# A gated cross-attention and int8 layer on one core: the order of the last step, and who makes the last batch's scales

## The reference, cut to what matters

```python
x = x + tanh(g_xattn) * cross_attention(layernorm(x), ctx)     # 16 batches, 512 rows of 512, 16 heads, 120 keys
# then, with layernorm(x) as z, row by row:
amax    = max(abs(z), axis=-1)
x_scale = maximum(amax, 1e-6) / 127
z_q     = round(z / x_scale)                                    # int8
ffn     = (z_q @ weight_q.T) * x_scale * weight_scale + bias
x = x + tanh(g_ffn) * ffn
```

## Time and profile before

| | |
|---|---|
| median of three executions | 811.59 us (811.49 to 811.66) |
| the profiled execution's own time | 812.33 us |
| its span | 810.4 us |
| PE busy | 794.0 us (98%) |
| DVE busy | 582.8 us (72%) |
| ACT busy | 556.1 us (69%) |
| POOL busy | 523.7 us (65%) |

### The profile page before, as it was taken

How to read it: one execution, slowest core, us unless ns; L and a number is a source line. 1 busy time by engine, 2 the same in 40 slices (tenths; PEclk the granted TensorE clock), 3 DMA queues, 4 the chain that set the end, 5 groups by cost and what they waited for, 6 DMA issues and landing times.

```text
span 810.4 us, 17171 instructions
## 1 busy us (share of the span) xinstructions
PE 794.0 (98%) x6658; PEld 522.4 (64%) x6658; DVE 582.8 (72%) x916; ACT 556.1 (69%) x845; POOL 523.7 (65%) x518
## 2 busy tenths in 40 slices
PE   8899999999999999999999999999999999999995
PEld 5665666666666766667667666667667666666563
DVE  4877788676767768678676767768578666767768
ACT  5676577675776667676676776667677675777685
POOL 4626484775947568494685947568495775845687
PEclk9999999999999999999999999999999999999999
DMA  8632604242141422314242161323414141111112
GB/s 278 231 69 90 200 28 124 73 154 75 40 160 62 137 79 72 125 53 142 74 140 70 41 186 53 118 80 82 133 54 123 61 117 54 53 40 53 53 52 104
DMA packets 39632, 79.68 MB, mean 98 GB/s; under 512 B 6913, under 2 KB 8321, under 8 KB 37505
## 3 DMA queue, kind: packets, MB, share of 16 engines
q1 hardware_dynamic: 38976, 77.75, 30.2%
q10 hardware_dynamic: 576, 0.85, 0.3%
HBM read 61.78 MB, written 16.81 MB: 97 GB/s over the span
## 4 chain that ended last, share of the span: by engine, by line
PE 88%; DVE 5%; issue 2%; POOL 1%; ACT 1%; DMA 1%; SPq 0%; DVEq 0%; ACTq 0%; POOLq 0%
PE bank_b L340 29%; PE bank_a L340 19%; PE scores L395 8%; PE sum_ps L426 7%; PE scores L412 7%; PE pv_ps L430 6%; PE bank_a L474 5%; PE scores L417 2%; PE bank_b L474 2%; DVE row_max L1092 2%; PE bank_a L449 1%; PE sum_ps L403 1%; DMA wk_stage<-in_wk 1%; DVE q_lo L1103 1%; PE scores L370 1%
## 5 line engine op out<-in xcount | busy, mean ns | idle before, releaser
L1092 DVE TENSOR_REDUCE row_max<-scores 128x16 f32<-128x1920 f32 x64 | 138.0, 2157 | 125.7 <-PE scores L395 125.7
L1433 POOL TENSOR_TENSOR o_lo<-on,o_hi 128x512 fp32r<-128x512 f32 x48 | 68.5, 1427 | 130.6 <-ACT o_hi L788 130.6
L770 ACT ACTIVATE probs<-scores 120x2048 f32<-120x2048 f32 x64 | 120.5, 1882 | 39.7 <-PE scores L417 39.7
L1441 POOL TENSOR_TENSOR x<-x,gbias_r 128x512 f32<-128x512 f32 x64 | 82.1, 1284 | 26.3 <-ACT cen L794 25.2
L395 PEld LDWEIGHTS scores<-k_sb,q_sb 32*128 32x128 f32 x2048 | 62.9, 186 | 53.0 <-issue 52.3
L1399 POOL TENSOR_TENSOR xt<-xt,rstd_b 128x512 f32<-128x512 f32 x60 | 91.4, 1571 | 2.4 <-ACT rstd_b L1026 2.1
L1429 POOL TENSOR_TENSOR x<-x,gbo_r 128x512 f32<-128x512 f32 x64 | 83.9, 1323 | 2.1 <-DMA x<-in_x 2.0
L788 ACT ACTIVATE o_hi<-on 128x512 fp32r<-128x512 f32 x48 | 30.3, 632 | 72.9 <-DVE on L1113 72.9
L340 PE MATMUL bank_b<-xt_hi,wq_hi 128*128 128x512 f32 x188 | 79.4, 422 | 0.5 <-DVE xt_lo L1082 0.5
L1446 POOL TENSOR_TENSOR x<-x,u_sb 128x512 f32<-128x512 f32 x56 | 73.6, 1315 | 7.9 <-DVE u_sb L1181 7.9
L395 PE MATMUL scores<-k_sb,q_sb 32*128 32x120 f32 x2048 | 74.7, 282 | 1.3 <-issue 0.9
(11 more groups left out here) (222 smaller groups left out, 1973.8 us busy)
## 6 DMA issues: line engine op xcount, KB each, us to landing
xt<-in_x_t SPq DMA_DIRECT2D x16, 1024.0 KB, 6.3
x<-in_x SPq DMA_DIRECT2D x64, 256.0 KB, 2.9
out_x<-x SPq DMA_DIRECT2D x61, 256.0 KB, 2.0
x_in<-in_x SPq DMA_DIRECT2D x60, 256.0 KB, 3.4
rstd_b<-rstd_rows SPq DMA_DIRECT2D x14, 256.0 KB, 4.7
ctx_sb<-in_ctx_t SPq DMA_DIRECT2D x8, 360.0 KB, 4.7
probs<-in_wq SPq DMA_DIRECT2D x4, 256.0 KB, 4.3
x<-in_wo SPq DMA_DIRECT2D x1, 1024.0 KB, 9.3
```

Source lines behind the costliest of these rows:

```text
L770: act.activation(probs[0:KEYS], scores[0:KEYS], ACT.Exp, scale=SCALE).then_inc(p_ready, 1)
L1092: dve.tensor_reduce(row_max[:].rearrange("p (t r) j -> p r t j", r=ROWG)[:, :, :, j], scores[:, :, 0:QT * KEYS].rearrange("p r (t k) -> p ...
L1433: pool.tensor_tensor(o_lo[i % 2][j], on[:], o_hi[i % 2][j].bitcast(F32), ALU.subtract).then_inc(o_split, 1)
L1441: pool.tensor_tensor(x1_of(m)[:, t], x1_of(m)[:, t], gbias_r[:], ALU.add).then_inc(x1b_ready, 1)
```

## The change

Five edits, all in the last step and in what follows it:

- PE: tile 1's chunk 2 moves from ahead of the wait for `o_last_split` to behind it; tile 0's chunk 3 is now the first work behind the wait, and then come tile 1's chunks 2 and 3.
- POOL, last step: `x1_deviations(m, 1)` is put ahead of `add_out(e, 3)`; `bias_x1(m, 3)` goes ahead of `bias_x(i, 2)`; `bias_x(i, 3)` leaves the step and is done behind `deviation_last(1)`.
- POOL makes one more value in `deviation_last`: `floor_last` = (var + eps) * rstd * 1e-6.
- DVE's `quant_factors_last` makes `q_unit` = max(amax, floor) / 127 and its reciprocal `q_rec`, two instructions for three.
- `xs_last` = q_unit * rstd * 127 is made by POOL in a new `unit_last`, for all four tiles between the last `bias_x1` and the first `add_own`.

```diff
--- before.py
+++ after.py
@@ -102,7 +102,7 @@
         x1_stat, x1_mv = sb("x1_stat", [P, QT, 6]), sb("x1_mv", [P, QT, 2])
         x1_var, x1_rstd, x1_std = sb("x1_var", [P, QT]), sb("x1_rstd", [P, QT]), sb("x1_std", [P, QT])
         q_amax, q_xs, q_unit, q_rec = (sb(f"q_{s}", [P, QT]) for s in ("amax", "xs", "unit", "rec"))
-        xs_last, rec_last = sb("xs_last", [P, QT]), sb("rec_last", [P, QT])
+        xs_last, floor_last = sb("xs_last", [P, QT]), sb("floor_last", [P, QT])
         cen = sb("cen", [P, 2, D + 1])
         u_sb = sb("u_sb", [P, D])
         z_b = [sb(f"z_b{i}", [P, D], BF16) for i in range(2)]
@@ -158,7 +158,7 @@
         ffn_done, u_ready = sem("ffn_done"), sem("u_ready")
         x1b_ready, out_ready = sem("x1b_ready"), sem("out_ready")
         o_last_split, last_pool, last_steps = sem("o_last_split"), sem("last_pool"), sem("last_steps")
-        last_xs = sem("last_xs")
+        last_xs, last_units = sem("last_xs"), sem("last_units")
         last_turned, last_zt, last_out = sem("last_turned"), sem("last_zt"), sem("last_out")
         last_stored = sem("last_stored")
 
@@ -630,12 +630,15 @@
                 pe.wait_ge(u_ready, nth(e, QT, 3))
                 turn_z(m, 0, bank_b)
                 pe.wait_ge(o_split, nth(i, DT, 2))
-                for t in range(2):
-                    for c in range(DT - 1):
-                        add_heads(i, t, c, scores[:, t])
+                for c in range(DT - 1):
+                    add_heads(i, 0, c, scores[:, 0])
+                for c in range(DT - 2):
+                    add_heads(i, 1, c, scores[:, 1])
                 pe.wait_ge(o_last_split, 1)
-                for t in range(2):
-                    add_heads(i, t, DT - 1, scores[:, t]).then_inc(proj_done, 1)
+                add_heads(i, 0, DT - 1, scores[:, 0]).then_inc(proj_done, 1)
+                for c in range(DT - 2, DT):
+                    ins = add_heads(i, 1, c, scores[:, 1])
+                ins.then_inc(proj_done, 1)
                 project_o(i, 2, scores[:, 2])
                 pe.wait_ge(log_done, nth(i, DT, 3))
                 turn_z(m, 1, sum_ps)
@@ -811,7 +814,7 @@
                                bias=x1_mv[:, t, 0:1]).then_inc(cen_ready, 1)
 
             def round_last(t):
-                act.wait_ge(last_steps, nth(t, 2, 1))
+                act.wait_ge(last_steps, t + 1)
                 act.activation(cen_last[t], cen_last[t], ACT.Identity, scale=q_rec[:, t:t + 1],
                                bias=magic[:]).then_inc(scaled, 1)
 
@@ -1150,13 +1153,11 @@
 
             def quant_factors_last(t):
                 one = slice(t, t + 1)
-                dve.wait_ge(last_pool, nth(t, 2, 1))
+                dve.wait_ge(last_pool, nth(t, 3, 2))
                 dve.wait_ge(amax_done, nth(LAST, QT, t))
-                dve.tensor_scalar(xs_last[:, one], q_amax[:, one], x1_rstd[:, one], Q_EPS, ALU.mult, ALU.max).then_inc(last_xs, 1)
-                dve.wait_ge(last_xs, t + 1)
-                dve.reciprocal(rec_last[:, one], xs_last[:, one]).then_inc(last_steps, 1)
-                dve.wait_ge(last_steps, nth(t, 2, 0))
-                dve.tensor_scalar(q_rec[:, one], rec_last[:, one], x1_rstd[:, one], Q_MAX, ALU.mult, ALU.mult).then_inc(last_steps, 1)
+                dve.tensor_scalar(q_unit[:, one], q_amax[:, one], floor_last[:, one], 1.0 / Q_MAX, ALU.max, ALU.mult).then_inc(last_units, 1)
+                dve.wait_ge(last_units, t + 1)
+                dve.reciprocal(q_rec[:, one], q_unit[:, one]).then_inc(last_steps, 1)
 
             def dequantise_own(m, t, bank):
                 dve.wait_ge(ffn_done, nth(m, QT, t))
@@ -1416,8 +1417,15 @@
                 one = slice(t, t + 1)
                 pool.wait_ge(x1_mean, nth(LAST, QT, t))
                 pool.tensor_scalar(x1_var[:, one], x1_mv[:, one, 1], LN_EPS, 1.0, ALU.add, ALU.mult).then_inc(last_pool, 1)
-                pool.wait_ge(last_pool, nth(t, 2, 0))
+                pool.wait_ge(last_pool, nth(t, 3, 0))
                 pool.tensor_tensor(x1_rstd[:, one], x1_var[:, one], half_neg[:, one], ALU.pow).then_inc(last_pool, 1)
+                pool.wait_ge(last_pool, nth(t, 3, 1))
+                pool.tensor_scalar(floor_last[:, one], x1_var[:, one], x1_rstd[:, one], Q_EPS, ALU.mult, ALU.mult).then_inc(last_pool, 1)
+
+            def unit_last(t):
+                one = slice(t, t + 1)
+                pool.wait_ge(last_units, t + 1)
+                pool.tensor_scalar(xs_last[:, one], q_unit[:, one], x1_rstd[:, one], Q_MAX, ALU.mult, ALU.mult).then_inc(last_xs, 1)
 
             def quant_units(m, h):
                 two = slice(2 * h, 2 * h + 2)
@@ -1523,24 +1531,26 @@
                 quant_units(m, 0)
                 bias_x(i, 1)
                 low_o(i, 2)
+                x1_deviations(m, 1)
                 add_out(e, 3)
-                x1_deviations(m, 1)
                 bias_x1(m, 2)
+                bias_x1(m, 3)
                 bias_x(i, 2)
                 quant_units(m, 1)
-                bias_x(i, 3)
-                bias_x1(m, 3)
 
             def turns_and_layers():
                 m = LAST - 1
                 deviation_last(0)
                 deviation_last(1)
+                bias_x(LAST, 3)
                 bias_x1(LAST, 0)
                 bias_x1(LAST, 1)
                 deviation_last(2)
                 deviation_last(3)
                 bias_x1(LAST, 2)
                 bias_x1(LAST, 3)
+                for t in range(QT):
+                    unit_last(t)
                 for t in range(QT):
                     add_own(m, t)
                 add_own(LAST, 0)
```

## The result

| | before | changed |
|---|---|---|
| median, 17 executions each | 811.54 us (810.77 to 814.51) | 813.33 us (812.2 to 816.31) |
| ratio, 95% interval | | 1.0026 (1.0016 to 1.0035), so +2.1 us (1.3 to 2.8) |
| the profiled execution's span | 810.4 us | 814.3 us |

The account below looks back on a forecast made before the run. PE bounds the whole (88%), but the end is the later of DVE's and POOL's last adds; POOL's was forecast at 808.92 against DVE's old 807.85, +1.07, rounded to +1.0: 811.59 + 1.0 = 812.6 us, range 811.1 to 813.6.

Parts of the forecast that it names:

- PE stands no more: Last step, PE ahead of o_hi_end: with 15 matmuls ahead it arrives at 785.69 and its 0.38 us wait is gone.
- the load goes out: SyncE's queue, x's tile 2: load moves from 783.28 to 785.04 behind the later store, so POOL starts at 787.85.
- All three of DVE's adds meet POOL's: Tail: each DVE add takes turns with a POOL add_own, each meeting costing POOL 0.44 us.
- rival 1: The forecast itself: in the tail POOL's chain ends last, +0.5 to +1.6 us; chance 0.62.
- the start of the adds: POOL's list in the tail: add_own was forecast to start at 801.37, where it was 800.23.
- the price of the floor: POOL's deviations in the tail: power to floor and the floor add 0.27 us, 1.19 from tile to tile.
- the 0.08 behind each pair of deviations: POOL's list in the tail: a 0.08 us step put between a pair of tiles' deviations and the next bias.
- the eight instructions: POOL's new floors and units for four tiles in the tail: forecast to cost 1.9 us by their starts.
- the four units with the step to the first add: End of POOL's list: four unit_last at 0.20 us each from 800.52, ending at 801.32, add_own at 801.37.
- rival 4: POOL's per-row scalar form is slow, deciding from some 0.36 us an instruction: slower by over 0.2%; chance 0.11.
- The load's lateness: Front of POOL's tail list: the load delayed like the store, starting POOL 1.76 us later, at 787.85 for 786.09.
- the time around the tail doesn't change: Outside the profiled span: 1.93 us lie around it and were taken not to change.

Follow-up runs that it names:

- e3: Changed kernel with the PE and POOL order edits undone, so only the new scales against the kernel before: median 814.28 us, ratio 1.0030 to the kernel before.
- e2: Kernel before with only the new order on PE and POOL, scales made as before: median 811.57 us, ratio 0.9989 to the kernel before.
- e1: The changed kernel measured again, unchanged: median 815.07 us, ratio 1.0043 to the kernel before.
- e4: Changed kernel with the last batch's tile 0 added by DVE, not POOL: median 813.37 us, ratio 1.0019 to the kernel before.
- e8: Changed kernel plus a main-loop POOL wait for DVE's q_lo, with add_out ahead of x1_deviations again: median 813.06 us, ratio 1.0015 to the kernel before.
- e7: Changed kernel plus a main-loop POOL wait for DVE's q_lo of chunk 3: median 812.92 us, ratio 1.0021 to the kernel before.

## Why the prediction was wrong

What was right, each time as the trace has it less 2.54 against the forecast: x1_deviations from 781.73 (781.71); low_o_last from 783.98 (783.97), ending at 785.20 (785.17); PE stands no more; the load goes out at 785.07 (785.04) and lets POOL start at 787.79 (787.85); q_unit of tile 0 at 790.65 (790.63). POOL is busy without a gap from there on; its adds start at 801.81 (801.37) and end at 809.31 (808.92); DVE's end is at 806.97 (about 806.5). All three of DVE's adds meet POOL's, as the forecast had it. The chain ends in POOL's add: the mechanism of rival 1, the forecast, is what the tail shows. e3 against e2 shows that the scales cost 1.26 and the order gives 0.90; together they give 1.37 and not 0.36. With the new scales the order gives nothing (811.80 for e3's 811.69), since POOL's list, longer and started later, sets the start of the adds, and with it the end.

**The first step that failed** is a size, the price of the floor: "Power to floor and the floor itself: 0.27 more". It took 0.37, a gap of 0.10 and the floor's 0.27; from one x_var to the next are 1.28 us and not 1.19. Four times 0.09 is 0.36, of the 0.44 us by which the start of the adds was missed; the four units with the step to the first add took 0.93 for a forecast 0.85. The forecast's list has two more slips, which nearly cancel: the 0.08 behind each pair of deviations is counted twice, and 0.08 ahead of each pair (x_var at 791.86 behind q_xs's end at 791.77, and at 798.28 behind a bias that ended at 798.19) is left out. In all the eight instructions cost POOL 2.4 us, 0.36 for a floor and 0.23 for a unit, for a forecast 1.9. That is also near rival 4's threshold, which was put too high: by the forecast's own prices a sum of +1.65 needs 0.32 an instruction and not 0.36; measured was 0.30 on the mean. The load's lateness was priced as a fixed 1.76, which is its usual size: its spread, 2.65 to 4.78, was not in the sum.

**The second step that failed** was taken at nothing without a reason: that the time around the tail doesn't change. The tail costs 1.37 of the 2.1 us. The executions on record show where the rest lies. In the first measurement 15 of 17 executions of the kernel before stand in one group, 810.8 to 811.7, and 9 of 17 of the changed kernel in another, 812.2 to 813.3. The medians of these two groups are 1.40 us apart, which is the tail; the other 2 and 8 executions lie at least 3.0 and 1.3 us above their group's median. So the remaining 0.7 us is that more executions of the changed kernel fell into the upper groups: 8 of 17 for 2 of 17 there, 9 of 12 for 17 of 35 in e1.

What single traces show of such steps is as large as the forecast: 1.6 us for a lost race between DVE's q_lo and POOL (e1 and e3, three times in e4; 0.5 for the one of 5.92 in the kernel before, at 114 us), 1.5 us for a stretch at the lower clock early on (e8, e2; twice that in the changed kernel's first trace), 1.4 to 1.8 us for a late load, which only the new order exposes. Why the changed kernel should meet them more often is not shown, and stays open. Both occur in kernels with and without the edits, and far ahead of the edited code. The mean clock of every execution is on record, 0.994 or less in 16 of 88 for kernels with the new scales and in 11 of 187 for those without, but it can't settle this: it includes the low clock at the end of the execution, 3.4 to 7.4 us in the traces with the new scales and 1.4 to 5.1 in the others (e7's trace has a mean of 0.996 with no early drop, e2's 0.997 with one).

The tail of 1.37 lies inside the measured interval, 1.3 to 2.8, at its low end; e1's interval starts at 1.0025, 2.0 us, above it. The change measured is above rival 1's +0.5 to +1.6, though its mechanism is what the tail shows. That the median, 813.33, lies within the stated range, up to 813.6, is luck: the range reached so far for the slow per-row form of rival 4, not for this.

## What to carry to other kernels

When two engines end within a microsecond of each other, work moved from one to the other is paid by the one that becomes the end; before moving it, walk that engine's whole list to its last instruction. And look whether the two ends are apart at all: here DVE's end followed POOL's by 0.55 us wherever it came last. Two edits in one change had opposite signs: tried apart, in the traces, the order was worth 0.9 us while the scales cost 1.3. A tiny instruction on POOL costs its span and the gaps around it, and a store delayed by POOL also delays the loads queued behind it, with all the spread of their landing. When executions fall into groups, compare group with group before giving the difference of medians to the code that was edited.

## What the runs showed of the hardware

- A DVE instruction with both inputs in SBUF does not always get its turn at the next change of POOL's instructions. At the same place it took 0.78 us in one execution and 6.99 in another, with five POOL instructions of 1.35 to 1.38 us run past it. The starts differed by little: DVE's request came 0.16 us ahead of POOL's next start in the one, 0.13 in the other. In e3 it lost with 0.16 too, so the lead alone doesn't decide. The Trainium skill ("SBUF — State Buffer", "Who interferes with whom") has it that issue order decides who blocks, and, of DVE's 2-port modes, that whoever issues first holds the pair for the whole instruction while the other blocks; here the trace shows DVE, which asked first, wait for five instructions that were issued behind it.
- The landing of a 256 KB load issued right behind a store ranged from 2.65 to 4.78 us over the nine traces with the late store; seven of them have 2.65 to 2.83.
- POOL's scalar instruction on 128x1 took 0.19 us with constants, and 0.27 with a per-row scalar, with a gap of 0.10 where it waited for the instruction before; in a row of four that wait for nothing such instructions start 0.23 to 0.24 apart.
